# A layer chain on one Trainium2 core: a group's rows turned, copied and split over two rounds of the light attention, and VectorE's routing sum ahead of a statistic

## The reference

```
def light_attn(x, ln_g, ln_b, w_qkv, w_out):
    xn = layernorm(x, ln_g, ln_b)
    q, k, v = jnp.split(xn @ w_qkv, 3, axis=-1)
    ...                       # 8 heads of 64; windows of 64 rows, each with
                              # its left and right neighbour
    sim = einsum('bhnwd,bhnWd->bhnwW', q * DH ** (-0.5), kk)
    attn = softmax(where(kmask, sim, -max), axis=-1)
    o = einsum('bhnwW,bhnWd->bhnwd', attn, vv)
    return o @ w_out

def coor_descent(s, k_eff):   # routing: 50 steps, 4 problems of 2048 scores
    a = logk - logsumexp(s + b);  b = -relu(s + a)
```

## Time and profile before

| what | us |
|---|---|
| median of three runs | 2570.76 (2564.38 to 2593.01) |
| the profiled execution's own time | 2565.56 |
| its span | 2563.8 |
| TensorE matmuls busy | 2275.8 (89%) |
| TensorE weight loads busy | 1596.4 (62%) |
| VectorE busy | 1910.8 (75%) |
| ScalarE busy | 1510.4 (59%) |
| GpSimd busy | 1332.7 (52%) |

### The profile page before, as it was taken

How to read it: one execution, slowest core, us unless ns; L and a number is a source line. 1 busy time by engine, 2 the same in 40 slices (tenths; PEclk the granted TensorE clock), 3 DMA queues, 4 the chain that set the end, 5 groups by cost and what they waited for, 6 DMA issues and landing times. The chain is left out here.

```text
span 2563.8 us, 48908 instructions
## 1 busy us (share of the span) xinstructions
PE 2275.8 (89%) x17037; PEld 1596.4 (62%) x17037; DVE 1910.8 (75%) x4315; ACT 1510.4 (59%) x3369; POOL 1332.7 (52%) x1271
## 2 busy tenths in 40 slices
PE   5869999999999987889999979999868998999697
PEld 2455656565656565567777746666645776777555
DVE  5999999999999998166676657888865555566545
ACT  6678887878787874333333225555545667655522
POOL 2887979797978785143333224445564233221411
PEclk8869998989998988999999989999988999999899
DMA  6445454444444443010000143343220000000300
GB/s 205 160 134 165 135 165 137 155 154 133 160 129 164 129 150 99 17 62 1 1 1 1 26 92 64 68 76 61 52 70 9 21 19 18 22 19 19 112 15 9
DMA packets 139461, 206.74 MB, mean 81 GB/s; under 512 B 24481, under 2 KB 59426, under 8 KB 139090
## 3 DMA queue, kind: packets, MB, share of 16 engines
q1 hardware_dynamic: 137234, 200.73, 26.7%
q0 software_dynamic: 960, 2.62, 0.3%
q10 hardware_dynamic: 1024, 0.26, 0.1%
HBM read 161.29 MB, written 14.68 MB: 69 GB/s over the span
## 5 line engine op out<-in xcount | busy, mean ns | idle before, releaser
L481 POOL TENSOR_TENSOR ma_seen<-ma_state,ma_cs 128x1024 f32<-128x1024 f32 x256 | 601.7, 2364 | 201.5 <-DVE ma_state L1157 148.7
L1157 DVE TENSOR_TENSOR_SCAN ma_state<-ma_decay,ma_last,ma_drive 128x512 f32<-128x512 f32 x512 | 628.5, 1263 | 30.6 <-ACT ma_decay L969 29.3
L969 ACT ACTIVATE ma_decay<-ma_dt,ma_a_neg 128x512 f32<-128x512 f32 x512 | 338.8, 711 | 0.9 <-DVE ma_dt L1227 0.6
L700 PEld LDWEIGHTS ma_acc<-ident,ma_seen 128*128 128x128 f32 x2048 | 249.9, 150 | 135.1 <-POOL ma_seen L481 72.1
L700 PE MATMUL ma_acc<-ident,ma_seen 128*128 128x128 f32 x2048 | 281.0, 289 | 58.3 <-POOL ma_seen L481 58.3
L1144 DVE TENSOR_TENSOR ma_drive<-ma_weight,ma_bs 128x512 f32<-128x512 f32 x512 | 325.2, 681 | 0.4 <-ACT ma_weight L956 0.4
L2292 DVE CUSTOM_DVE_ANT_0 sw_score<-sw_score,both_band 128x256 f32<-128x256 f32 (+1 forms) x512 | 197.5, 448 | 49.8 <-PE sw_score L2106 38.9
L104 POOL TENSOR_TENSOR moe_h_low<-both_V,light_wqkv 128x512 fp32r<-128x512 f32 x80 | 105.0, 1312 | 247.4 <-DVE light_wqkv L100 239.9
L2230 ACT ACTIVATE sw_prob<-sw_turned 128x512 f32<-128x512 f32 (+1 forms) x256 | 135.5, 581 | 158.8 <-PE sw_turned L2120 132.6
L2028 POOL TENSOR_SCALAR_AFFINE_SELECT sw_prob<-sw_prob 128x512 f32<-128x512 f32 x128 | 84.4, 660 | 189.3 <-ACT sw_prob L2230 189.3
L1752 DVE TENSOR_TENSOR both_V<-both_V,moe_up 128x512 f32<-128x512 f32 x80 | 55.0, 688 | 120.6 <-PE moe_up L1541 75.3
(11 more groups left out here) (591 smaller groups left out, 5755.8 us busy)
## 6 DMA issues: line engine op xcount, KB each, us to landing
ma_bs<-bc_rows SPq DMA_DIRECT2D x256, 256.0 KB, 3.3
ma_cs<-bc_rows SPq DMA_DIRECT2D x256, 256.0 KB, 3.2
ma_h<-kept_taps SPq DMA_DIRECT2D x28, 256.0 KB, 4.9
both_wide<-both_kh SPq DMA_DIRECT2D x28, 192.0 KB, 4.6
both_wide<-both_qh SPq DMA_DIRECT2D x20, 256.0 KB, 4.6
x_rows<-X SPq DMA_DIRECT2D x1, 4096.0 KB, 14.3
light_rows<-li_y SPq DMA_DIRECT2D x32, 128.0 KB, 1.7
out_dram<-li_o SPq DMA_DIRECT2D x32, 128.0 KB
```

The lines of the kernel that those rows point to most:

```text
L481: g.tensor_tensor(out=seen[n % RR][:, :, :], in0=state[n % SR][:, :, :], in1=each(cs[n % CR][:, :], 2), op=ALU.mult).then_inc(S["seen_full ...
L700: ins = t.matmul(accs(j, mm), seen[n % RR][:, mm, j * P:(j + 1) * P], K["ident"][:, :], is_transpose=True, start=False, stop=(last_ and j ...
L969: a.activation(decay[s % DR][:, :], dt[:, m, :], ACT.Exp, scale=a_neg[:, m, k:k + 1]).then_inc(S["decay_done"], 1)
L1157: v.tensor_tensor_scan(state[n % SR][:, mm, :], decay[s % DR][:, :], drive[mm][:, :], last[:, k, m:m + 1], ALU.mult, ALU.add).then_inc(S[" ...
```

## The change

Three edits. First, `light_ahead` gives the first half of a group's `xT` to the round without a unit and leaves the second half where both were, for groups 2 to 7 (group 1 keeps both in one call ahead of the loop). The four transposes, ScalarE's copy, VectorE's split, ScalarE's copy of the high part and GpSimd's low part move with the half. Second, the helpers `x_lows` and `x_highs` take the halves that they are to make as an argument. Third, on VectorE `route_sum` stands ahead of `zstats`. No instruction is added or taken away, no DMA is moved, and the order of the units in the two banks stays.

```diff
@@ light_ahead
-        if at == 0:
+        if j == 1 and at == 0:
             found += [("xT", j, m) for m in range(DH)]
+        if j > 1 and at in (-1, 0):
+            found.append(("xT", j, at + 1))
@@ gpsimd
-            def x_lows(j):
-                for hh in range(DH):
+            def x_lows(j, halves):
+                for hh in halves:
...
-                    if (kind, m) == ("xT", 0):
-                        x_lows(j)
+                    if kind == "xT":
+                        x_lows(j, (m,))
@@ scalar, copies
-                    if j and m == DH - 1:
+                    if j and (j > 1 or m == DH - 1):
                         act.wait_ge(S["v_full"], GT * j)
-                        for hh in range(DH):
+                        for hh in range(DH) if j == 1 else (m,):
                             act.wait_ge(S["x_cut"], DH * (j - 1) + hh + 1)
@@ vector
-            def x_highs(j):
+            def x_highs(j, halves):
...
-                for hh in range(DH):
+                for hh in halves:
...
-                        x_highs(unit[1])
+                        x_highs(unit[1], (unit[2],))
...
+                if R_ < FIRST_DIGIT:
+                    route_sum(R_ + OPENING)
                 if r == 0 and 0 <= n - 2 < TILES:
                     zstats(n - 2)
-                if R_ < FIRST_DIGIT:
-                    route_sum(R_ + OPENING)
```

More of the change, by code:

```diff
@@ L2808, in _ @@
             pool.wait_ge(S["w_in"], LOADED)
-            x_lows(1)
+            x_lows(1, range(DH))
             for R_ in range(HALVES + 4):
@@ L3742, in _ @@
                     route_move(5)
-            x_highs(1)
+            x_highs(1, range(DH))
             dve.wait_ge(S["made"], made_steps[1])
```

## The result

The changed kernel takes 2588.16 us, median of 20 runs (2577.56 to 2610.14), against 2573.39 us of the kernel before, median of 20 runs beside it (2556.83 to 2594.8). The ratio is 1.0062 with a 95% interval of 1.0036 to 1.0088: 16 us slower (9 to 23). 2582 us was forecast, with a range of 2569 to 2593. Kernels are compared here by these ratios, since a single execution of either kernel can come out 20 us from the median.

What follows compares the result with a forecast made beforehand. TensorE bounds most of the 64 rounds, in lockstep with VectorE and ScalarE in rounds like 14 and 15. 10.8 + 2.2 + 2.4 + 2.1 - 2.2 = +15.3 us on 2565.56 gave 2580.9, forecast as 2582, range 2569 to 2593.

Steps and rivals of the forecast that it cites:

- the split waits for ScalarE's copy: Round 14, VectorE: the split ahead of `shifts` waits for ScalarE's copy of the first half, so `shifts` start 2.4 us later.
- the cast beside the low part: Round 14: GpSimd's low part holds one step of VectorE's `shifts`, subtraction or cast, by 0 to 1.06 us, taken as 1.0.
- the slow clock: TensorE's 3.5 us idle in round 14 may halve its clock: 0 to 1.2 us a group, taken as 0.35, +2.1 in all.
- VectorE's delay: Rounds 14 and 15: `maxes` 3.4 us later, less 0.7 us of ScalarE copy, make `project` 2.7 us later; +10.8 over four groups.
- no or a shorter collision: Rival: GpSimd's low part holds VectorE's `shifts` for less or not at all; 2574 us, chance 0.14.
- the one in which VectorE's wait costs nothing: Rival: VectorE's wait is free, so TensorE keeps the saved transposes and waits; 2554 us, faster, chance 0.09.
- the one in which the half does not move up: Rival: bank or V copies late in round 14, so TensorE or ScalarE waits longer; part of the upper end, no separate chance.
- The swap: Routing sum ahead of statistics on VectorE: sum 0.56 us sooner, -2.2 us in rounds 4, 12, 20, 28, 36; nothing in rounds without units.
- The slow-clock rival: Rival: TensorE's slow clock lasts through each `xT` round and into the next; 2587 to 2592 us, chance 0.19.
- The wait ahead of `project`: Round 15: TensorE waits for ScalarE's `li_xT` copy until 2073.1, hiding 1.5 us of the slow clock's cost.
- Group 5: Rounds 30 and 31: `project` already began 0.7 us behind the copies, so the delay adds only 2.2 us.
- Group 7: Rounds 46 and 47: second sum of counts 3.4 us later, less 1.0 us of transposes gone, +2.4 us.

Runs made afterwards that it cites:

- the low part later: Changed kernel with GpSimd making both low parts in the `xT` round; rounds 14 and 15 took 13.74 us, all rounds 461.3, one run 2572.36 us.
- all splitting later: Changed kernel with only the first half's transposes and ScalarE's copy of them early, all splitting in the `xT` round; rounds 14 and 15 11.48 us, ratio 0.9974.
- the split behind `shifts`: Changed kernel with VectorE's early split placed after `shifts` in the same round; rounds 14 and 15 took 12.65 us, one run 2570.76 us.
- 8 products: Changed kernel with 8 unread TensorE products before the routing sum in rounds 6, 14, 22, 38; rounds 14 and 15 took 14.84 us, one run 2577.04 us.
- 13 products: Changed kernel with 13 unread TensorE products before the routing sum in rounds 6, 14, 22, 38; rounds 14 and 15 took 16.24 us, one run 2582.70 us.
- both halves early: Changed kernel with both halves' transposes and ScalarE's `xT` copies a round early, all splitting one round behind; rounds 14 and 15 9.81 us, ratio 0.9933.

## Why the prediction was right, step by step

For a pair of rounds like 14 and 15:

| step | foretold | measured | by |
|---|---|---|---|
| one ScalarE copy fewer in the `xT` round | -0.7 | -0.71 | 12.19 to 11.48 |
| the split waits for ScalarE's copy | +2.4 | +2.27 | 11.48 to 13.75 |
| the cast beside the low part | +1.0 | +1.09 | 13.75 to 14.84 |
| the slow clock | +0.35 | +0.72, mean of four | 14.84 to 14.86 ... 16.16 |

- **VectorE's delay** was right in size and in kind: 14.84 - 12.19 = 2.65 us against 2.7. Counted from the start of round 14, `shifts` came 2.27 us later, where 2.4 were foretold, and `maxes` 3.4 us, as foretold. TensorE's wait came out at 3.61 us for 3.5. With the clock the pair grew by 3.5 us, more than the 2.5 to 3 that the prediction's list of signs gave. The rivals with no or a shorter collision, and the one in which VectorE's wait costs nothing, fell here. So did the one in which the half does not move up: its copy started at 2079.63, 3.4 us into round 14, the moment at which the prediction had ScalarE free.
- **The first subtraction was not held**, only the cast. The prediction had left open which; the sum had one held step either way.
- **The swap** gave 0.48, 0.50, 0.50 and 0.49 us in the round pairs 4+5, 12+13, 20+21 and 36+37, and 0.50 in 28+29: 2.5 us for the 2.2 foretold.
- **The clock was the term that was mis-sized.** I took 0.35 us in a group from bounds of 0 to 1.2; the four pairs show 0.02 to 1.32, mean 0.72. The mistake was to start from round 14 before, which kept the full clock beside short waits, when the 3.5 us wait resembled round 30, which did not. The slow-clock rival took 1.2 us; the mean lies between the two, a little nearer to 0.35, and two of the four pairs (1.32 and 0.88) lie nearer to the rival.
- **The wait ahead of `project`** was foretold for round 15 and isn't in the changed kernel. It is there (1.46 to 1.48 us) at full clock in the kernels with the low part later, with all splitting later, with the split behind `shifts` and with 8 products; with 13 products, which delay TensorE itself, it is 0.94 us. At half clock TensorE's own work fills the time until ScalarE's copy is done. So 1.5 us of what the low clock costs are hidden, as the prediction had it.
- **Group 5** cost 18.34 - 16.78 = +1.6 us, foretold +2.2 and the clock. That is near, but for a reason that the prediction had not: it said that the swap gives nothing in a round without a unit. Without the swap the early split made this pair 19.89 us, +3.1, with more of it at the low clock (0.74 in place of 0.81 as a mean); with the swap alone it took 15.71 us, 1.1 less than before, and TensorE's wait of 1.15 us for the sum was gone. In that kernel the low clock also came sooner (round 30's scores took 1.56 us in place of 0.88), so what of the 1.1 us is the swap and what the clock is not separated.
- **Group 7** cost 20.85 - 18.34 = +2.5 us, foretold +2.4. This closeness is partly luck: the same instructions of this pair took 18.34 and 19.23 us in the kernel before and in that with the swap alone, and 20.85 and 19.88 us in the changed kernel and in those with products added elsewhere.
- **The sum**: the four pairs +13.5 (12.2 foretold with the clock), group 5 +1.6, group 7 +2.5, the swap -2.5; that is +15.1 of the 14.7 measured. Two differences that nobody foretold nearly cancel: rounds 26 and 27 +1.3 us, rounds 60 and 61 -1.2 us. So the sum is nearer to its forecast than its terms are: too little for the clock was made up for by less in group 5 and more from the swap.
- **The time in us** is another matter. 2588 against 2582 is 6 us off, while the difference to the kernel before was right within 1 us: the forecast counted from about 2567 us, and the kernel before had a median of 2573.39 us in the runs beside it.

The longer rounds 26 and 27 are a matter of the clock. They took 18.4 to 18.8 us in the three kernels in which the granted clock was 0.91 there (the changed one, the swap alone, both halves early) and 17.1 to 17.2 us in the seven in which it was 1.00. Before, and with the swap alone:

```profile
2143.20:2160.35 17.15, 14.44 (x198) 11.16 (x197) 7.71 (x32) 13.07 (x42) 5.79 (x12) 1.00 0.06 18
2170.05:2188.79 18.74, 16.10 (x198) 12.25 (x197) 7.72 (x32) 13.05 (x42) 5.76 (x12) 0.91 0.05 17
```

What stays open: why the low clock covers more of one pair than of another in one execution (it makes 14.86 or 16.16 us of the same instructions), why it came in rounds 26 and 27 in three kernels only, and what shortens rounds 60 and 61, where TensorE waits 4.83 us for ScalarE's `li_prob` before and 2.84 us after.

A second limit is the scale of the measurement. Over the ten profiled executions round 0 starts between 1962 and 1992 us, behind parts that no kernel here changes. That is twice the effect in question, so one run's time can't judge any of these kernels. The stretch of all rounds in one trace is better, but it moves by 1 to 2 us with the clock in single pairs. What holds to a few hundredths of a us is a pair at full clock, four times in each trace; the explanation rests on those.

## What to carry to other kernels

VectorE ran its instructions in the program's order in every trace here. On such an engine an instruction moved earlier brings its wait along, and everything behind it pays: here 0.43 us of work cost 2.27 us a group, because the steps that others wait for stood behind it. Before moving a step up, move what feeds it, and let the step itself stay where its input is surely there; the kernel with both halves early does that and is the only one whose time is clear of the kernel before, by 0.7%. And price the wait that you create by what it does to TensorE's clock too: take the nearest stretch with an idle time of that length, not the nearest in place, and give it a range, since the same wait of 3.6 us cost 0.02 to 1.32 us.

## What the runs showed of the hardware that I had not expected

- A cast of 128x16 that starts beside GpSimd's subtraction of two 128x512 operands lasts as long as that: 1.27 us for 0.17 (2081.13 + 1.27 against 2081.10 + 1.27). A subtraction of 128x8 that started 0.17 us ahead of the low part took its usual 0.16 us. With the split behind `shifts`, the statistics and the maxima ran beside such a low part and kept 0.41 and 1.02 us. The Trainium skill (VectorE: DVE Perf Modes, "Two Vector instructions with no wait between them") tells of a read interface that VectorE shares with GpSimd in a two-port mode or with two inputs; the trace agrees in that the statistics and maxima, which have one input each, kept their time. In which mode the cast ran, the trace does not show. The hold lasted to the end of GpSimd's instruction.
- The low clock costs anything from 0.02 to 1.32 us at the same place of the same program, four times in one execution. The granted clock is then 0.78 to 0.89 as a mean of the pair. With a wait of 2.5 us and 0.88 in three of four pairs it cost nothing, since a later wait of 1.47 us took it up. With TensorE kept busy through the wait the clock was 1.00, and the four pairs agreed within 0.02 us.
